# Attention and feed-forward kernel: batch 0's operand stacks loaded in three parts, with prologue and first-period work moved

## The reference

```
scores = alpha * tanh(q k / beta) + lam * (tanh(x hex) . tanh(x hex)) / 2
         + lattice term from tanh(x q6), one 6x6 map per head
attn   = softmax(causal scores);   x1 = layernorm(x + (attn v) out_w)
r = sigmoid(xr W_r);  k = relu(xk W_k)^2;  out = layernorm(x1 + r * (k W_v))
```

## Time and profile before

| | |
|---|---|
| median of 3 runs | 407.52 us (407.02 to 409.52) |
| profiled execution | 406.31 us, span 404.6 us |
| PE, DVE, ACT, POOL busy | 89%, 82%, 81%, 57% of the span |
| DMA over the span | 53.74 MB, mean 133 GB/s |

### The profile page before, as it was taken

How to read it: one execution, slowest core, us unless ns; L and a number is a source line. 1 busy time by engine, 2 the same in 40 slices (tenths; PEclk the granted TensorE clock), 3 DMA queues, 4 the chain that set the end, 5 groups by cost and what they waited for, 6 DMA issues and landing times.

```text
span 404.6 us, 8754 instructions
## 1 busy us (share of the span) xinstructions
PE 358.2 (89%) x2907; PEld 197.6 (49%) x2907; DVE 333.6 (82%) x536; ACT 327.6 (81%) x367; POOL 229.8 (57%) x367
## 2 busy tenths in 40 slices
PE   2857959889999999999999999999989998999863
PEld 1232425345655564655564556555634564446452
DVE  3763877979999999989999999999978967896734
ACT  1122459989998999899999999899989998999621
POOL 4314353665577658765777567956793636353632
PEclk9999969999999999999999999999999999999978
DMA  4177777657633576357535764575347631010000
GB/s 115 29 221 198 223 206 193 170 169 203 162 102 114 153 199 177 96 163 190 164 119 140 181 162 136 150 194 163 91 137 201 166 88 31 23 28 1 2 28 26
DMA packets 37483, 53.74 MB, mean 133 GB/s; under 512 B 3396, under 2 KB 35140, under 8 KB 35866
## 3 DMA queue, kind: packets, MB, share of 16 engines
q1 hardware_dynamic: 32585, 50.83, 45.2%
q10 hardware_dynamic: 4865, 2.49, 2.5%
HBM read 38.69 MB, written 14.61 MB: 132 GB/s over the span
## 4 chain that ended last, share of the span: by engine, by line
PE 58%; ACT 13%; DVE 12%; issue 7%; POOL 4%; DMA 3%; SPq 1%; POOLq 0%; DVEq 0%; ACTq 0%
PE raw L515 27%; PE side_bank L515 15%; PE sums L515 12%; ACT probs L806 6%; ACT probs L811 5%; DVE probs L1050 5%; PE side_bank L605 4%; DMA k_rows<-parts 2%; POOL parts L951 2%; POOL res L979 1%; DMA probs<-in_L_attn_hex_w 1%; DVE bn L1135 1%; ACT k_act L823 1%; DVE mean_var L1142 1%; DVE bn L1337 0%
## 5 line engine op out<-in xcount | busy, mean ns | idle before, releaser
L1050 DVE SCALAR_TENSOR_TENSOR probs<-probs,scal,raw 128x1024 f32<-128x1024 f32 x160 | 202.2, 1274 | 25.7 <-PE raw L515 25.2
L806 ACT ACTIVATE probs<-raw 128x1024 f32<-128x1024 f32 x160 | 165.1, 1032 | 24.6 <-PE raw L515 22.4
L811 ACT ACTIVATE probs<-probs 128x1024 f32<-128x1024 f32 x160 | 170.4, 1067 | 0.3 <-DVE probs L1050 0.3
L938 POOL TENSOR_SCALAR_AFFINE_SELECT probs<-probs 128x256 f32<-128x256 f32 (+1 forms) x224 | 97.7, 452 | 104.3 <-ACT probs L811 103.5
L515 PE MATMUL raw<-q_stack,k_stack 72*128 72x384 bf16 (+3 forms) x512 | 98.7, 306 | 12.6 <-DVE probs L1050 11.7
L515 PE MATMUL raw<-i_stack,j_stack 111*128 111x384 bf16 (+3 forms) x512 | 98.2, 304 | 3.8 <-ACT probs L806 3.8
L515 PE MATMUL sums<-probs,values 128*32 128x256 f32 (+2 forms) x1280 | 82.3, 384 | 0.4 <-POOL probs L938 0.4
L515 PEld LDWEIGHTS raw<-q_stack,k_stack 72*128 72x128 bf16 x512 | 42.7, 99 | 63.2 <-DVE probs L1050 31.2
L515 PEld LDWEIGHTS raw<-i_stack,j_stack 111*128 111x128 bf16 x512 | 41.7, 98 | 46.5 <-ACT probs L806 16.9
L515 PEld LDWEIGHTS sums<-probs,values 128*32 128x32 f32 x1280 | 33.7, 109 | 29.4 <-issue 19.5
L951 POOL TENSOR_TENSOR parts<-whole,parts 128x512 bf16<-128x512 f32 x30 | 35.8, 1201 | 12.7 <-DVE parts L1089 12.0
(11 more groups left out here) (150 smaller groups left out, 345.7 us busy)
## 6 DMA issues: line engine op xcount, KB each, us to landing
q_stack<-q_rows SPq DMA_DIRECT2D x21, 384.0 KB
k_stack<-k_rows SPq DMA_DIRECT2D x21, 384.0 KB
i_stack<-lattice_i SPq DMA_DIRECT2D x21, 288.0 KB
i_stack<-hamming_i SPq DMA_DIRECT2D x21, 288.0 KB
q_rows<-parts SPq DMA_DIRECT2D x8, 384.0 KB, 4.3
k_rows<-parts SPq DMA_DIRECT2D x8, 384.0 KB, 2.6
k_rows<-parts SPq DMA_DIRECT2D x8, 256.0 KB, 2.9
x_res<-in_L_attn_x SPq DMA_DIRECT2D x8, 256.0 KB, 3.0
```

The source lines that it names most:

```text
L806: nc.scalar.activation(pair_probs(t), raw[:, t % PSUM_PAIRS, :].rearrange("p (u i) -> p u i", u=2), ACT.Tanh).then_inc(tanh_done, 1)
L811: nc.scalar.activation(pair_probs(t), pair_probs(t), ACT.Exp).then_inc(exp_done, 1)
L938: last = nc.gpsimd.affine_select(out=v, in_=v, compare_op=ALU.is_ge, fill=0.0, base=0, pattern=[[0, v.shape[1]], [1, P]], channel_multipli ...
L1050: v.scalar_tensor_tensor(out=o, in0=o, scalar=scal[:, 2:3], in1=raw[:, t % PSUM_PAIRS, :].rearrange("p (u i) -> p u i", u=2), op0=ALU.mult ...
```

## The change

Batch 0's stacks now come in heads 0 to 3, 4 to 7 and 8 to 15. On SP batch 1's Q and K rows are written between the second and the third part, and its J and G rows behind the third. PE gets `busy(n)`, n products of the identity with itself into an unused bank, at eight places of the prologue (43 in all). `late_weights` moves ahead of scores (0,0); k2, scores (0,1) and F2 follow; G for batch 1 moves behind the start of period 0. DVE's and POOL's steps for batches 1 and 2 get new places in period 0.

```diff
-FIRST_UNITS = ["xT1", "F1", "q1", "k0", "G1", "v1", "xT2", "q2", "k2", "F2", "G2"]
-LATE_WEIGHTS = 3
+FIRST_UNITS = ["xT1", "F1", "q1", "k0", "G1", "v1", "xT2", "q2", "k2", "F2"]
+SECOND_UNITS = {1: ["G1"], 2: ["xT2"], 3: ["q2"], 4: ["k2"], 6: ["F2"], 7: ["v1"], 13: ["G2"]}
 def units_at(t, post, prep, values):
+    if not post:
+        return SECOND_UNITS.get(t, [])
...
 # SP
-            def write_rows(n, par):
-                for kind in (Q, K, J, G):
+            def write_rows(n, par, kinds=(Q, K, J, G)):
+                for kind in kinds:
...
+                    sp.wait_ge(second_in, 16 * (STACK_DMAS[Q] + STACK_DMAS[K] + STACK_DMAS[G]))
...
                 for kind in (Q, K, G):
-                    load_stack(sp, kind, 0, stack_in[kind], (4, H))
-                write_rows(1, 1)
+                    load_stack(sp, kind, 0, second_in, (4, 8))
+                write_rows(1, 1, (Q, K))
+                for kind in (Q, K, G):
+                    load_stack(sp, kind, 0, stack_in[kind], (8, H))
+                write_rows(1, 1, (J, G))
 # PE
+                elif first and t == PAIRS_PER_QUAD:
+                    pe.wait_ge(second_in, 16 * (STACK_DMAS[Q] + STACK_DMAS[K] + STACK_DMAS[G]))
-                elif t == (PAIRS_PER_QUAD if first else 0):
+                elif t == (2 * PAIRS_PER_QUAD if first else 0):
...
+            def busy(n):
+                for _ in range(n):
+                    mm(sums[:, 0:P], ident[:], ident[:])
             pe.wait_ge(s_ident, 1)
+            busy(8)
             side(-1, "xT1")
+            busy(6)
...
             transposed(raw[:, 0], [w_nat[:, n, :] for n in (0, 1, 7, 2)]).then_inc(s_wT, 1)
+            busy(4)
             pe.wait_ge(s_dve0, DVE0_FEATURES)
             side(-1, "F1")
+            busy(3)
...
             side(-1, "k0")
+            busy(2)
             pe.wait_ge(s_dve0, DVE0_LATTICE)
             side(-1, "G1")
+            busy(4)
...
             side(-1, "v1")
+            busy(12)
             side(-1, "xT2")
+            busy(4)
             side(-1, "q2")
+            late_weights()
+            scores(0, 0, 0)
             side(-1, "k2")
+            scores(0, 0, 1)
             side(-1, "F2")
-            scores(0, 0, 0)
-            scores(0, 0, 1)
-            side(-1, "G2")
 # ACT, period
                     tanh(b, t)
+                    if n_is(b, 0) and t == 0:
+                        side(-1, "F2")
...
-            side(-1, "F2")
 # POOL
+            FIRST = {1: [(lo, 1, Q)], 2: [(rest, 1, J), (rest, 1, G)], 3: [(lo, 1, K)], 4: [(lo, 1, J)],
+                     6: [(lo, 1, G)], 7: [(rest, 2, Q)], 9: [(rest, 2, K)], 11: [(lo, 2, Q)],
+                     13: [(lo, 2, K), (rest, 2, J)], 14: [(rest, 2, G)], 17: [(lo, 2, J)], 18: [(lo, 2, G)]}
...
-            lo(1, Q)
-            rest(1, J)
-            lo(1, K)
-            rest(1, G)
-            lo(1, J)
-            lo(1, G)
 # DVE
-            FIRST = {0: [(mid, 1, K)], 1: [(mid, 1, J), (wo_heads,)], 3: [(mid, 1, G)], 4: [(late_weights,)]}
+            FIRST = {0: [(hi, 1, J), (mid, 1, Q)], 1: [(features_i, 1), (hi, 1, G)], 2: [(mid, 1, K), (x_out, 2)],
+                     3: [(projected, 2, Q), (mid, 1, J)], 4: [(projected, 2, K)], 5: [(mid, 1, G)], 6: [(hi, 2, Q)],
+                     7: [(values_in, 1)], 8: [(hi, 2, K)], 10: [(mid, 2, Q)], 12: [(mid, 2, K), (hi, 2, J)],
+                     13: [(features_i, 2), (hi, 2, G)], 16: [(mid, 2, J)], 17: [(mid, 2, G)]}
...
             x_out(1)
+            wo_heads()
             projected(1, Q)
             hi(1, Q)
+            late_weights()
             projected(1, K)
             hi(1, K)
-            hi(1, J)
-            mid(1, Q)
-            features_i(1)
-            hi(1, G)
```

More of the change, by code:

```diff
@@ L126, in made @@
             return self.through(-1, "k0")
-        if use == "v" or n_is(n, 0):
+        if use == "v" or n_is(n, 0) or n_is(n, 1) and use == "G":
             return self.through(n - 1, use + "1")
@@ L145, in before @@
         last = self.uses(b - 1 if isinstance(b, int) else b)[-1]
-        assert last not in ACT_UNITS
-        return False, self.start(b, False)
+        return last in ACT_UNITS, self.start(b, last in ACT_UNITS)
 def build(nc, x, qkv_w, out_w, hex_w, lam_logit, q6_w, transforms, transform_weights, scale_logit,
@@ L293, in build @@
         stack_in = [sem(f"stack_in{n}") for n in range(4)]
-        first_qk, first_g = sem("first_qk_in"), sem("first_g_in")
+        first_qk, first_g, second_in = sem("first_qk_in"), sem("first_g_in"), sem("second_in")
         xres_in = sem("xres_in")
@@ L630, in side @@
                 elif use in ("G1", "G2"):
-                    pe.wait_ge(act_freed, side_units.through(b, "F" + use[-1]))
+                    pe.wait_ge(act_freed, side_units.made(b + int(use[-1]), "F"))
                     last = mm(o, lat_map[:], feats[:])
@@ L685, in period @@
                         side(b, use)
-                    if not post and t == LATE_WEIGHTS:
-                        late_weights()
                     if post:
@@ L979, in gated_residual @@
                 nc.gpsimd.tensor_tensor(res[:], gated[:], x1[:], ALU.add).then_inc(gate_done, 1)
+            FIRST = {1: [(lo, 1, Q)], 2: [(rest, 1, J), (rest, 1, G)], 3: [(lo, 1, K)], 4: [(lo, 1, J)], 6: [(lo, 1, G)], 7: [(rest, 2, Q)],
+                     9: [(rest, 2, K)], 11: [(lo, 2, Q)], 13: [(lo, 2, K), (rest, 2, J)], 14: [(rest, 2, G)],
+                     17: [(lo, 2, J)], 18: [(lo, 2, G)]}
             PREP = {5: [(rest, K)], 6: [(rest, Q)], 14: [(lo, Q), (rest, G)], 16: [(rest, J)], 17: [(lo, K)],
@@ L988, in period @@
                         mask(*lagged(b, t, EXP_LAG))
-                    for stage, *a in PREP.get(t, []) if prep else []:
+                    for stage, *a in FIRST.get(t, []) if not post else []:
+                        stage(*a)
+                    for stage, *a in PREP.get(t, []) if post and prep else []:
                         stage(b + 2, *a)
@@ L1178, in period @@
                         stage(*a)
-                    if values and t in VALUES_UNITS:
+                    if post and values and t in VALUES_UNITS:
                         values_in(b + 1)
@@ L1182, in period @@
                         stage(b - 1, *a)
-                    for stage, *a in SPLIT.get(t, []) if prep else []:
+                    for stage, *a in SPLIT.get(t, []) if post and prep else []:
                         stage(b + 2, *a)
```

## The result

| | before | after |
|---|---|---|
| median | 408.52 us (4 runs beside) | 405.28 us (400.62 to 407.19, 4 runs) |
| ratio | | 0.9896, interval 0.9851 to 0.9941 |
| again, beside e10 and e11 (e9) | 408.04 us | 405.20 us, 0.9905 (0.9863 to 0.9947) |
| profiled execution | 406.31, span 404.6 | 407.19, span 405.5 |

The change gains about 1%, 4 us; the forecast was 1 us, within 1%. The profiled execution is 1.6% above the fastest of the four and is left out of the ratio, and its profile shows no gain at the end. It is still the one to read first, since it shows where a gain of 14 us turned into nothing; the profiles of e1 (404.63 us) and e9 (403.82 us) show the same wait.

A forecast was written before the change was run, and what follows sets the result against it. Early ACT starvation, PE's low clock and SP's DMA queue were taken to bound it. Stacks in at 85.3, plus 1.2 for the clock, less 87.6, gave -1.1 us: 406.4 against the median 407.5, range 401 to 411.

The forecast's parts named there:

- all three parts: ACT starving ahead of tanh (0,7), PE's low clock early, and SP's DMA queue with 6.4 us slack at biases (1,0).
- signs of being right: Tanh (0,0) near 32, (0,7) at 50 to 52, idle before biases (1,0), DMA ending 83 to 87, clock low some 5 us.
- sign of being wrong: Biases (1,0) without a wait, a period 0 hole over 1 us before scores or biases (0,10), or a later batch period differing.
- The limit at batch 1: Batch 1's stacks in at 85.3, pairs wanting them at 77.2, so biases (1,0) wait 8 us.
- lo(1,K): POOL's lo of batch 1's K, which the third part waits for: taken at 43.6, bounds 42.5 and 49.5.
- the third part's 10.5 us: Load of batch 0's last stacks, 2016 KB at 192 GB/s, starting at lo(1,K) + 2.7 = 46.3.
- Cost of splitting: Twelve more DMAs: some 24 us if paid in series; the forecast used 0.76 us of issue each, overlapped with data.
- 0 between -0.5 and +1.0: Early gain in us from the identity products ahead of 26.8, DVE being held busy until the values of batch 0.
- The clock after the wait: PE's clock falls in the wait at batch 1, returns 5.0 us after work resumes; net cost +1.2 us.
- The sum: At biases (1,0): 85.3 + 1.2 - 87.6 = -1.1 us; bounds -6.4 and +4.8.
- the first rival: The queue keeps up, stacks moving faster beside idle engines: -4 to -8 us, around 401.5; chance 0.27.
- the clock stays low in the prologue: Rival: lo(1,K) comes at 49.5, SP waits with its queue empty, time 412.3 us; chance 0.16.

The follow-up runs named there:

- e10: e5 without the identity products, so the new order of steps with the loads of the kernel before: 404.38 us, ratio 0.9886.
- e11: e8 without the identity products: 397.48 us, ratio 0.9733 to the kernel before.
- e9: The changed kernel run again, unaltered: 405.20 us, ratio 0.9905 to the kernel before.
- e1: Control: the changed kernel with PE's periods 1 and 2 written out ahead of its loop: 403.32 us, ratio 0.9858 to the kernel before.
- e3: e1 with batch 1's stacks loaded in two parts, heads 0 to 3 first: 397.96 us, ratio 0.9745 to the kernel before.
- e7: The kernel before with batch 1's stacks loaded in two parts, heads 0 to 3 first: 408.05 us, ratio 1.0013.
- e4: The changed kernel without its identity products: 405.87 us, ratio 0.9956 to the kernel before.
- e5: The changed kernel without the third part: heads 4 to 15 in one part, then batch 1's rows: 401.49 us, ratio 0.9842 to the kernel before.
- e2: e1 with 32 identity products keeping PE busy in the wait ahead of biases (1,0): 401.08 us, ratio 0.9838 to the kernel before.
- e6: The kernel before with the change's identity products at the same places up to q2, nothing else: 405.99 us, ratio 0.9962.
- e8: e3 with batch 3's hi of Q and K on DVE, and their rest on POOL, later in period 1: 396.10 us, ratio 0.9721.

## Why the prediction held

**What bounds.** Right in all three parts. The pace per batch stayed (tanh (2,0) to (3,0) takes 42.0 us, before and after), the 4 us hole went, and the slack of 6.4 us at biases (1,0) is what the gain ran into. Of the signs of being right, three did not come: tanh (0,7) is at 46.4, not at 50 to 52; the share of DMA does not fall to nothing at 83 to 87 but is 0.82 there; and the clock is low for 9.4 us, not for some 5. One sign of being wrong did come, an idle stretch above 1 us ahead of biases (0,10): it is 1.42 us long.

**The limit at batch 1.** Right, shown by e3 and by e7: with the bytes sooner, 5 us more; before the change, nothing. The stacks were forecast in at 85.3, pairs wanting them at 77.2; they were in at 83.4 and wanted at 76.0. The forecast came from SP's order: lo(1,K) at 43.6 was 39.4, and the third part's 10.5 us were nearer 13, from lo(1,K) + 2.7 = 42.1 to biases (0,10) at 55.2. SP's timeline:

```profile
38.55 0.47 SPq L366 DMA_DIRECT2D q_rows<-parts  x1
39.40 0.36 SPq L369 DMA_DIRECT2D k_rows<-parts  x1
...
40.44 2.56 SPq L387 DMA_DIRECT2D q_stack<-q_rows  x3
...
51.91 2.28 SPq L387 DMA_DIRECT2D q_stack<-q_rows  x3
...
71.61 1.91 SPq L366 DMA_DIRECT2D q_rows<-parts  x1
...
80.54 0.75 SPq L376 DMA_DIRECT2D hamming_i<-parts  x1
```

Three issues take 2.2 to 2.6 us for 96 KB as for 288, as taken. Batch 1's stacks start 1.2 us sooner than before and still end later, at 83.4: 29.8 us from their first data and not 26.4. The prediction counted no other bytes in that stretch. The last two rows are batch 2's rows, 1.5 MB issued from 71.6 to 81.3, so ahead of 83.4; before, only their Q part (77.2) was issued ahead of 83. The DMA engines moved 5.9 MB in these 29.8 us and 4.9 MB in the 26.4. That the rows delayed the stacks fits this, but no run holds them back to show it.

**Cost of splitting.** The Trainium skill ("DMA: Bandwidth & Descriptors", section Bandwidth) has the rule to batch DMAs to a megabyte. The Trainium skill (same page, section "Anatomy of one DMA") gives each a fixed part near 2 us, for DMAs issued by GpSimd; ours leave from SP. Paid in series, that is an estimate of 24 us for twelve more DMAs. The runs do not show it: e7 adds these twelve to the kernel before, where nothing is gained by them, and costs 0.5 us, at most 1.6 by its interval, and e3 is 5 us faster than its control.

**The prologue.** The step that failed is "0 between -0.5 and +1.0" for the identity products ahead of 26.8. DVE was held to be busy without a break up to the values' copy, and so to set it. It is busy so only from q1 on (11.7 us before and after); the start of that chain waits for q1, which PE now runs at the high level and 2.4 us sooner. DVE's and PE's timelines after, beside the earlier trace rows:

```profile
12.70 0.75 DVE L1092 TENSOR_SCALAR whole<-raw,cols 128x512 f32<-128x512 f32 x1 [0.36 <-PE raw L521]
...
23.65 0.76 DVE L1120 COPY values<-side_bank 128x256 f32<-128x256 f32 x2
```

```profile
1.59 3.79 PE L521 MATMUL sums<-ident 128*128 128x128 f32 x16 [1.59 <-POOL ident L937]
...
9.45 1.02 PE L521 MATMUL side_bank<-xT,w_fT 128*128 128x512 f32 x2
...
20.09 2.84 PE L521 MATMUL sums<-ident 128*128 128x128 f32 x24
```

With the eight products at the start the clock was up at 7.6 us, ahead of F1, not at q1 or k0, and the values' copy ended 2.4 us earlier. I had also priced an identity product by a transpose. A product takes 3.79/8 = 0.47 us low and 2.84/12 = 0.24 high, not 0.27 and 0.15. So the twelve behind v1 lasted until 22.9, PE idled 1.5 us and not 2.4, and the clock stayed up.

**The clock after the wait.** The mechanism was right, the size was off. Forecast: up again 5.0 us after work resumes, net +1.2. Measured: 9.4, 9.1, 2.9 and 3.8 us in four profiles (after, e1, e9, e4). What was lost from biases (1,0) to tanh (2,0), against before, is 4.5, 4.3, 1.4 and 1.8 us. The rows of before held one such recovery in the middle of the kernel, and I took it for the value.

**The sum.** -1.1 us forecast, about -4 measured. By its terms, in the profile after: lo(1,K) came 4.2 us earlier (2.4 by the prologue, 1.1 taken for a low clock in xT2 to k2 that did not come, the rest not traced); batch 1's stacks started another 1.1 earlier, ahead of the end of the third part; they took 3.4 longer. That gives 83.4 and not 85.3. The clock's term is 4.5 there and not 1.2, which makes 83.4 + 4.5 - 87.6 = +0.3; in e9 it is 82.2 + 1.4 - 87.6 = -4.0. So some 5 us of errors one way met 2 to 7 us the other way. That the time came out inside a range ten us wide was partly their cancelling, which is luck; -4.2 by the ratio also lies in the band of the first rival, -4 to -8.

**The rivals.** That the queue moves the stacks faster beside idle engines did not occur: they took 29.8 us and not 26.4, and the third part 13 and not 10.5. That the clock stays low in the prologue did not occur; e4 made it occur, and it cost 2 us and not 6, since the third part started 3.2 us later there and biases (1,0) only 1.1.

## What to carry to other kernels

Before a stall is removed, look for the next resource with little slack behind it and count its bytes to that point: here 14 us won in the prologue and the first pairs met 6.4 us of slack in a DMA queue that had not been empty from 31 to 81 us. Then order the queue by what the consumer needs first in every batch that is loaded in a hurry, not in the first alone. Count with them the next batch's bytes that come forward too. And if a stall can't be removed, it may be cheaper in a stretch that still has time to spare: e5's 7 us in period 0 against the changed kernel's at batch 1 is the one case of it here.

## What the runs showed of the hardware

- With eight identity products from 1.6 us on, and PE's work behind them, its clock was up at 4.7 to 7.6 us in the eight profiles with them (after, e1, e2, e3, e5, e6, e8, e9). Without them (before, e4, e7, e10, e11) it first rose at 31 to 47 us.
- The column PEclk reads 1.00 ahead of the first rise, in the kernel before too; only the durations (2.04 us for a product that takes 1.08 later) tell the level there.
- One wait of PE in the same kernel was followed by 2.9 us or by 9.4 us at 1.2 GHz. The changed kernel's executions spread over 400.6 to 408.3 us. Without the wait e8 stays within 394.5 to 396.6, but e3 spreads over 395.8 to 400.1 and e11 over 395.7 to 399.4, so the wait is not the only source.
- The clock also fell with PE at work and no wait above 1 us just ahead: it was low in the changed kernel at 69.0 to 72.4 (in e9 at 70.9 to 74.9), in e1, e2 and e3 near 39 to 42.5, and in e10 at 75.9 to 82.7, where e10 fell 2.5 us further behind e5.
- SP takes about 0.75 us to issue one of these stack DMAs, whether it moves 72, 96 or 288 KB, as long as little is queued: the last of batch 1's took 9.8 us, with all the others ahead of it.
